# A graph network kernel on one core: 45 of the 99 groups of its dense stage moved beside two other stages

## The chip, the cores and the metric

The kernel runs on one core of a Trainium2 chip. The metric is the device time of one execution, in microseconds. The core has TensorE (PE, matmuls, and PEld, its weight loads), VectorE (DVE), ScalarE (ACT), GpSimd (POOL), SyncE (SP, which here only issues transfers) and 16 DMA engines. TensorE's clock has two levels, 1.2 and 2.4 GHz; the profile gives the granted clock as a share of the higher one.

## The reference

x holds 100,000 nodes of 64 features; 50,000 edges lead from src to dst, sorted by dst. Four layers follow one another, each of the form x = x + layer(relu(layernorm(x))):

- L0: attention with a weight matrix per node type and per edge type, softmax over the edges of a dst.
- L1: `relu(h_diff @ W_ffn.T + b_ffn)`, where h_diff sums differences of neighbours, gated by a cosine similarity, over edges.
- L2: `relu((h + agg) @ W0 + b0) @ W1 + b1` with a hidden width of 128.
- L3: attention over four heads, an output projection, `h @ Wf + bf`, and a layer norm with gamma and beta, added.

In each layer only nodes with an incoming edge receive a sum over edges; every other node gets what its own row gives. The kernel splits the work that way.

## The kernel before

The nodes, padded to 101,376, are 99 groups of 1024 rows; the padded edges are 99 groups of 512. Stages follow one another with a barrier between them: tables, dense, scores, softmax, attend, difference, propagate, mlp, heads. Each stage is a software pipeline written out per engine: in step n an engine works on group n for one operation and on group n - 1, n - 2 and so on for later ones (`st.back(lag)`). The order on each engine is the program's order; nothing reorders it. Buffers mostly come in threes (`U = 3`).

**dense** (L484) computes all layers for every node as if it had no edges, reads x and writes the normalized rows h2 and h3 (tables U2 and U3) and the output. Of a group, 128 partitions hold 8 rows of 64 each. The steps of group d: Pool adds the L1 bias row (x2, L517) and the L2 bias row (x2b, L520); VectorE sums and centers x2; ScalarE squares with an accumulator, row by row (L173), and takes the root; VectorE scales (h2, L193). TensorE turns h2 by four transposes (L655), ScalarE copies them to SBUF (L630), TensorE multiplies by w0, 64 rows of the array for each of two halves (the hidden layer, L673), ScalarE applies relu over both halves in one operation (L644), TensorE multiplies by w1 (m, L688). Two groups later: x3 = m + x2b (L582), normalized to h3, turned, copied (L633), multiplied by wf2 (h, L680, two column blocks per row); four groups later VectorE adds bias rows, normalizes and writes x4 (L565 to L613), with Pool's x3b (L530). Pool also scatters 396 index columns into the node table T0 there (L523), four per step.

**difference** (L1230), step n: Pool gathers four index columns of 128 rows (L1222). TensorE: p of group n - 2 (L1384), b of n - 2 (L1388, transposes), t of n (L1395, transposes of the gathered rows), c of n - 2 (L1401, eight passes of one column). VectorE: diff of n - 1 (L1298), lastv of n (L1304), the two scans (L1308, L1314), prod of n - 1 (L1318). ScalarE: relu of p, a square, a copy of b, a square, a copy of c. There are three PSUM banks for t.

**propagate** (L1409), step n: Pool gathers four columns (L1222), with a memset of a scratch tile between gathers (L1227). TensorE: t of n - 1 (L1528), f of n - 3 (L1533), x of n - 5 (L1538). VectorE: sum of n - 6, scan of n - 2 (L1473), centering, x2 of n - 4 (L1484), sum of squares, gating of n (L1491), reciprocal, scaling. ScalarE: square, root, relu of f, a store. There are three banks each for t and x.

TensorE, SP and Pool wait through a helper that is the same everywhere:

```python
def wait(eng, sem, value, passed=None):
...
    if isinstance(value, int) and value <= 0:
        return
    eng.wait_ge(sem, value)
```

## Time and profile before

| | us |
|---|---|
| median of 3 runs (6725.3 to 6734.1) | 6727.01 |
| the profiled execution | 6730.3 |
| its span, first to last instruction | 6728.5 |
| TensorE busy in the span | 5032.8 |
| VectorE busy | 4925.5 |
| Pool busy | 4927.1 |
| ScalarE busy | 2275.3 |

The profile is of one execution. A row of windows gives the stretch (us from the span's start), its length, the busy time of each engine with the number of instructions in parentheses, then the granted clock, the mean busy share of the DMA engines and GB/s. Where a row is of TensorE alone, only its busy time stands. A row of the timeline gives start, duration, engine, line, operation, tiles (out<-in), shapes, and in brackets the idle time before it with what ended it; for TensorE the shape 64*128 64x512 means 64 rows and 128 columns of the array and 512 moving columns. An fp32 matmul shows as two passes. A row of groups gives busy us, mean ns of one, and the idle time before. Starts that are closer than durations mean that operations overlap in their pipeline. No engine is busy over the whole span, so the table says little by itself; the stages have different limits.

### The profile page before, as it was taken

To read this page: it belongs to the slowest core of one execution; us is meant where nothing else is said; L and a number is where in the kernel's file an instruction comes from. 1 tells how busy PE (TensorE), PEld (TensorE's weight loads), DVE (VectorE), ACT (ScalarE), POOL (GpSimd) and SP (SyncE) were. 2 spreads that over 40 slices of the span, in tenths; PEclk is the share of its full clock that TensorE was granted. 3 is DMA by queue.
4 is the path that set the end of the run, shared out by engine and by line. 5 is a ranking of instruction groups with operands and counts; after the bars stand their busy time and mean duration, and the time that the engine had idled before them with its cause. 6 is when DMAs were issued, how large, how long until landed. Compare 5 with 4: busy or idle time off the path is not lost. (4 is left out here: it accounts for less than half of the span.)

```text
span 6728.5 us, 70067 instructions
## 1 busy us (share of the span) xinstructions
PE 5032.8 (75%) x17065; PEld 2608.6 (39%) x17065; DVE 4925.5 (73%) x7942; ACT 2275.3 (34%) x5856; POOL 4927.1 (73%) x5468
## 2 busy tenths in 40 slices
PE   0777777588888886888887888555578878788787
PEld 0455555344444442333334444122233334444443
DVE  4899999766676666999996666565567757666666
ACT  0555555322222222433332333121122223333333
POOL 1777777688888883666667887887677757777777
PEclk9877777799999997888885555555578867666666
DMA  9222222233333333555543333344455542222221
GB/s 350 88 95 95 95 95 95 78 75 78 74 79 74 78 75 81 142 145 143 145 130 83 83 82 77 93 109 102 100 136 144 146 119 62 65 65 65 62 61 42
DMA packets 788906, 673.39 MB, mean 100 GB/s; under 512 B 514176, under 2 KB 520906, under 8 KB 788376
## 3 DMA queue, kind: packets, MB, share of 16 engines
q1 hardware_dynamic: 486456, 459.62, 23.5%
q0 software_dynamic: 102464, 90.84, 8.5%
q10 hardware_dynamic: 199584, 118.45, 5.7%
q8 instruction: 145, 2.38, 0.1%
q14 instruction: 257, 2.11, 0.1%
HBM read 396.20 MB, written 276.35 MB: 100 GB/s over the span
## 5 line engine op out<-in xcount | busy, mean ns | idle before, releaser
L736 POOL DMA_INDIRECT sc_xg<-t,keep_gather x792 | 910.7, 1150 | 165.4 <-issue 146.4
L1222 POOL DMA_INDIRECT df_hs<-u,keep_idx x396 | 512.3, 1294 | 129.2 <-issue 108.3
L1222 POOL DMA_INDIRECT hd_gat<-u,keep_idx x396 | 478.5, 1208 | 161.6 <-issue 119.6
L1755 POOL DMA_INDIRECT out_x<-hd_x,keep_scat_out x396 | 458.1, 1157 | 151.4 <-issue 125.4
L1222 POOL DMA_INDIRECT ml_gat<-u,keep_idx x396 | 403.8, 1020 | 168.3 <-issue 70.0
L523 POOL DMA_INDIRECT t<-keep_ptr_pay,keep_scat_ptr x396 | 441.0, 1114 | 108.3 <-issue 106.1
L1222 POOL DMA_INDIRECT pr_gat<-sd,keep_idxsd x396 | 412.5, 1042 | 130.7 <-issue 69.4
L1198 PE MATMUL at_ps_m<-at_vx,keep_weights 128*64 128x512 f32 x792 | 447.3, 718 | 26.0 <-POOL at_vx L1095 26.0
L688 PE MATMUL den_ps_m<-keep_weights,den_hid 128*128 128x64 f32 x1584 | 243.8, 318 | 207.9 <-ACT den_hid L644 207.9
L876 PE MATMUL sc_ps_q<-sc_ht,keep_weights 128*128 128x512 f32 x396 | 272.7, 827 | 140.1 <-issue 84.9
L882 PE MATMUL sc_ps_r<-sc_qx,keep_weights 128*64 128x512 f32 x792 | 376.0, 619 | 1.0 <-DVE sc_prod L799 1.0
L1210 PE MATMUL at_ps_y<-keep_weights,at_agg 64*128 64x256 f32 x792 | 242.0, 456 | 170.8 <-DVE at_ysel L1122 170.6
L1095 POOL TENSOR_TENSOR at_vx<-at_eq,at_v 128x1024 f32<-128x1024 f32 x99 | 256.7, 2594 | 133.8 <-issue 81.2
L1895 PE MATMUL hd_ps_h<-keep_weights,hd_xb 128*128 128x128 f32 x792 | 249.3, 415 | 126.5 <-DVE hd_wn L1838 118.6
L150 DVE TENSOR_REDUCE sc_sc_n_sum<-sc_xg 128x8 f32<-128x512 f32 x99 | 67.9, 686 | 367.4 <-DMA sc_xg<-t,keep_gather 367.4
L154 DVE SCALAR_TENSOR_TENSOR den_den_n_cent<-den_den_n_sum,den_x 128x512 f32<-128x512 f32 x198 | 334.0, 1687 | 3.6
L655 PE MATMUL den_ps_t<-keep_consts,den_h 128*128 128x128 f32 x792 | 181.9, 380 | 197.0 <-DVE den_h L193 196.7
L688 PEld LDWEIGHTS den_ps_m<-keep_weights,den_hid 128*128 128x128 f32 x1584 | 228.3, 229 | 249.6 <-ACT den_hid L644 249.5
L1083 POOL TENSOR_TENSOR at_y<-at_ysel 128x512 f32<-128x512 f32 x99 | 137.3, 1387 | 245.4 <-DVE at_ysel L1122 245.4
L173 ACT ACTIVATE den_den_n_sq<-den_den_n_cent 128x64 f32<-128x64 f32 x792 | 190.6, 242 | 327.9 <-DVE den_den_n_cent L154 327.9
L1895 PEld LDWEIGHTS hd_ps_h<-keep_weights,hd_xb 128*128 128x128 f32 x792 | 196.7, 305 | 248.6 <-DVE hd_wn L1838 189.5
L833 ACT COPY sc_kv<-sc_ps_kv 128x512 f32<-128x512 f32 x99 | 58.1, 587 | 681.5 <-PE sc_ps_kv L888 672.9
(291 smaller groups left out, 13804.1 us busy)
## 6 DMA issues: line engine op xcount, KB each, us to landing
u<-den_h SPq DMA_DIRECT2D x198, 256.0 KB
t<-tab_row ACTq DMA_DIRECT2D x99, 272.0 KB, 11.3
tab_x<-in_x SPq DMA_DIRECT2D x99, 256.0 KB
den_x<-in_x SPq DMA_DIRECT2D x99, 256.0 KB
out_x<-den_x SPq DMA_DIRECT2D x99, 256.0 KB, 2.6
sc_et<-in_etype_row SPq DMA_DIRECT2D x99, 256.0 KB
at_v<-vt SPq DMA_DIRECT2D x198, 128.0 KB
at_et<-in_etype_row SPq DMA_DIRECT2D x99, 256.0 KB
```

Of the source, the lines that this page charges most:

```text
L154: v.scalar_tensor_tensor(out=self.cent[:, :, :], in0=self.over(self.sum), scalar=-1.0 / D, in1=x, op0=ALU.mult, op1=ALU.add).then_inc(self ...
L523: pool.indirect_dma_start(pairs, bass.IndirectOffsetOnAxis(ap=e.scat_ptr[:, c:c + 1], axis=0), e.ptr_pay[:, c, :], None, bounds_check=NP * ...
L688: m = pe.matmul(ps_m[:, j, :], hid[:, a, c * P:(c + 1) * P], e.W["w1"], start=(j == 0), stop=(j == RN - 1), skip_group_check=True)
L736: pool.indirect_dma_start(xg[i][:, u, :], None, e.T0, bass.IndirectOffsetOnAxis(ap=e.gather0[:, b.n, u:u + 1], axis=0), bounds_check=NP - ...
L876: m = pe.matmul(ps_q[:, :], e.W["q"][:, c * P:(c + 1) * P], ht[:, c, :], start=(c == 0), stop=(c == 1))
L882: m = pe.matmul(ps_r[:, :], e.W["att"][:, r * D:(r + 1) * D], qx[:, r, :], start=(r == 0), stop=(r == 3))
L1095: pool.tensor_tensor(vx[i][:, 2:4, :], eq[i][:, :, :], vin[i][:, :].unsqueeze(1).broadcast_to([P, 2, GE]), ALU.mult).then_inc(vx_high, 1)
L1198: m = pe.matmul(ps_m[d.s][:, :], e.W["msg"][:, r * D:(r + 1) * D], vx[d.s][:, r, :], start=(r == 0), stop=(r == 3))
L1210: m = pe.matmul(ps_y[:, u, :, :], agg[f.s][:, u * P:(u + 1) * P], e.W["a"][0:D, :].rearrange("p (t f) -> p t f", t=4), start=(u % 2 == 0), ...
L1222: pool.indirect_dma_start(gat[i][:, u, :], None, table, bass.IndirectOffsetOnAxis(ap=idx_all[:, c:c + 1], axis=0), bounds_check=rows - 1, ...
L1755: pool.indirect_dma_start(e.out, bass.IndirectOffsetOnAxis(ap=e.scat_out[:, c:c + 1], axis=0), x4[i][:, u, :], None, bounds_check=NP - 1, ...
L1895: pe.matmul(ps_h[i][:, u, :], xb[i][:, u * P:(u + 1) * P], e.W["wfx"], start=(u == 0), stop=False, skip_group_check=True)
```

## The change

Dense becomes a class whose work per group is cut into four parts per engine, with an own order of operations. It runs alone for 54 groups; 22 groups run beside difference and 23 beside propagate, one part per step of the host, at the end of each engine's step; what is left over runs after the host's last step. Pool has no arithmetic in dense: x2 and x2b go to VectorE; x3b and the bias of h's first block become matmuls with one row (`ones[0:1]` by `bias_h`) ahead of each half of h. VectorE sums the squares of x2; ScalarE squares in one wide operation and scales the rows of h2 and h3 by eight narrow operations each. The hidden layer has a bank per half. Beside a host (`tight`) both halves share one bank, as do the turns of h2 and h3. Difference and propagate keep one bank for t (and x) in place of three, so their waits go by the group before, not by the third before. In difference b, c and n share a bank. Pool's scatters spread over 54 steps, each let go by x2 of the step before; the memsets in propagate are gone.

```diff
+IN_DF = 22
+IN_PR = 23
...
+        dense(nc, e, NG - IN_DF - IN_PR)
...
+        difference(nc, e, NG - IN_DF - IN_PR, IN_DF)
+        propagate(nc, e, NG - IN_PR, IN_PR)
...
+                    link(v.tensor_copy(e.bias_h[0:1, :, half, :], bias[0:1, :].unsqueeze(1).broadcast_to([1, TU, D])))
...
+class Dense:
...
+    def __init__(self, s, e, first, count, tight=False):
...
+        self.ps_t2 = s.ps("dt2", [P, GE])
+        self.ps_t3 = self.ps_t2 if tight else s.ps("dt3", [P, GE])
+        self.ps_hid = [s.ps("dhid0", [P, GE])]
+        self.ps_hid.append(self.ps_hid[0] if tight else s.ps("dhid1", [P, GE]))
+        self.ps_m, self.ps_h = s.ps("dm", [P, RN, D]), s.ps("dh", [P, RN, 2, D])
...
+    def steps(self):
+        return self.count + 4
...
+    def vector(self, v, st, part):
+        e, d, f, g = self.e, st, st.back(2), st.back(4)
+        n2, n3, n4 = self.n2, self.n3, self.n4
+        if part == 0:
+            if self.on(f):
+                v.wait_ge(self.m_ready, f.n + 1)
+                v.wait_ge(self.x2b_done, f.n + 1)
+                wait(v, self.hx_done, f.n - (U - 1))
+                v.tensor_tensor(self.x3[f.s][:, :, :], self.ps_m[:, :, :], self.x2b[f.s][:, :, :], ALU.add).then_inc(self.x3_done, 1)
+            if self.on(g):
+                n4.sumsq(v, g)
+            if self.on(f):
+                v.wait_ge(self.x3_done, f.n + 1)
+                n3.total(v, self.x3[f.s][:, :, :]).then_inc(n3.chain, 1)
+            if self.on(d):
+                v.wait_ge(self.x_in[d.s], 16 * (d.k + 1))
+                v.tensor_tensor(self.x2[:, :, :], self.xin[d.s][:, :, :], self.rows(e.relu_b[:, :]), ALU.add).then_inc(self.x2_done, 1)
+        if part == 1:
+            if self.on(f):
+                v.wait_ge(n3.chain, 2 * f.n + 1)
+                wait(v, self.h3_done, f.n)
+                n3.shift(v, self.x3[f.s][:, :, :])
+            if self.on(g):
+                v.wait_ge(self.h_ready, g.n + 1)
+                wait(v, self.x4_done, g.n)
+                v.tensor_tensor(self.hx[:, :, :], self.ps_h[:, :, 1, :], self.x3[g.s][:, :, :], ALU.add).then_inc(self.hx_done, 1)
+                v.wait_ge(n4.rooted, g.n + 1)
+                v.reciprocal(n4.rstd[:, :], n4.std[:, :]).then_inc(n4.chain, 1)
+            if self.on(d):
+                v.wait_ge(self.x2_done, d.n + 1)
+                n2.total(v, self.x2[:, :, :]).then_inc(n2.chain, 1)
+            if self.on(g):
+                v.wait_ge(n4.chain, g.n + 1)
+                v.tensor_tensor(self.f1[:, :, :], self.ps_h[:, :, 0, :], n4.over(n4.rstd), ALU.mult).then_inc(self.f1_done, 1)
+        if part == 2:
+            if self.on(f):
+                n3.sumsq(v, f)
+            if self.on(d):
+                wait(v, self.x3_done, d.n - (U - 1))
+                v.tensor_tensor(self.x2b[d.s][:, :, :], self.x2[:, :, :], self.rows(e.W["b1_row"]), ALU.add).then_inc(self.x2b_done, 1)
+                v.wait_ge(n2.chain, 2 * d.n + 1)
+                wait(v, self.h2_done, d.n)
+                n2.shift(v, self.x2[:, :, :])
+            if self.on(f):
+                v.wait_ge(n3.rooted, f.n + 1)
+                v.reciprocal(n3.rstd[:, :], n3.std[:, :]).then_inc(n3.chain, 1)
+        if part == 3:
+            if self.on(g):
+                v.wait_ge(self.f1_done, g.n + 1)
+                v.tensor_tensor(self.f1[:, :, :], self.f1[:, :, :], self.rows(e.W["gamma"]), ALU.mult).then_inc(self.g1_done, 1)
+            if self.on(d):
+                n2.sumsq(v, d)
+            if self.on(g):
+                v.wait_ge(self.g1_done, g.n + 1)
+                v.wait_ge(self.hx_done, g.n + 1)
+                wait(v, self.x4_out[g.s], 16 * g.k)
+                v.tensor_tensor(self.x4[g.s][:, :, :], self.f1[:, :, :], self.hx[:, :, :], ALU.add).then_inc(self.x4_done, 1)
+            if self.on(d):
+                v.wait_ge(n2.rooted, d.n + 1)
+                v.reciprocal(n2.rstd[:, :], n2.std[:, :]).then_inc(n2.chain, 1)
+
+    def scalar(self, a, st, part):
+        e, d, f, g, d1, f1 = self.e, st, st.back(2), st.back(4), st.back(1), st.back(3)
+        eps = e.C["eps"]
+
+        def scale_rows(n, h, b, out, done):
+            a.wait_ge(n.chain, 2 * b.n + 2)
+            wait(a, out[b.s], 16 * b.k)
+            for j in range(RN):
+                m = a.activation(h[b.s][:, j, :], n.cent[:, j, :], ACT.Relu, scale=n.rstd[:, j:j + 1])
+            m.then_inc(done, 1)
+
+        if part == 0:
+            if self.on(g):
+                a.wait_ge(self.h_ready, g.n + 1)
+                wait(a, self.n4.summed, g.n)
+                a.activation(self.n4.sq[:, :, :], self.ps_h[:, :, 0, :], ACT.Square).then_inc(self.n4.squared, 1)
+                self.n4.root(a, g, eps)
+        if part == 1:
+            if self.on(f):
+                self.n3.square(a, f)
+            if self.on(d1):
+                a.wait_ge(self.t2, d1.n + 1)
+                a.copy(self.h2t[:, :], self.ps_t2[:, :]).then_inc(self.t2_kept, 1)
+            if self.on(f1):
+                a.wait_ge(self.t3, f1.n + 1)
+                a.copy(self.h3t[:, :], self.ps_t3[:, :]).then_inc(self.t3_kept, 1)
+        if part == 2:
+            if self.on(f):
+                self.n3.root(a, f, eps)
+            if self.on(d1):
+                for half in range(2):
+                    a.wait_ge(self.hid_ready, 2 * d1.n + half + 1)
+                    a.activation(self.hid[:, half, :], self.ps_hid[half][:, :], ACT.Relu, bias=e.W["b0"]).then_inc(self.hid_kept, 1)
+            if self.on(d):
+                self.n2.square(a, d)
+        if part == 3:
+            if self.on(f):
+                scale_rows(self.n3, self.h3, f, self.h3_out, self.h3_done)
+            if self.on(d):
+                self.n2.root(a, d, eps)
+                scale_rows(self.n2, self.h2, d, self.h2_out, self.h2_done)
+
+    def tensor(self, pe, st, part):
...
+        if part == 0:
+            if self.on(d):
+                wait(pe, self.h2_done, d.n + 1, passed)
+                wait(pe, self.t2_kept, d.n, passed)
+                if self.tight:
+                    wait(pe, self.t3_kept, f.n, passed)
+                turn(self.ps_t2, self.h2[d.s]).then_inc(self.t2, 1)
+        if part == 1:
+            if self.on(f):
+                wait(pe, self.h3_done, f.n + 1, passed)
+                wait(pe, self.t3_kept, f.n, passed)
+                if self.tight:
+                    wait(pe, self.t2_kept, min(d.n + 1, self.count), passed)
+                turn(self.ps_t3, self.h3[f.s]).then_inc(self.t3, 1)
+        if part == 2:
+            if self.on(d):
+                wait(pe, self.t2_kept, d.n + 1, passed)
+                for half in range(2):
+                    if self.tight:
+                        wait(pe, self.hid_kept, 2 * d.n + half, passed)
+                    else:
+                        wait(pe, self.hid_kept, 2 * (d.n - 1) + half + 1, passed)
+                    pe.matmul(self.ps_hid[half][:, :], e.W["w0"][64 * half:64 * half + 64, :],
+                              self.h2t[64 * half:64 * half + 64, :], start=True, stop=True).then_inc(self.hid_ready, 1)
+            if self.on(f):
+                wait(pe, self.t3_kept, f.n + 1, passed)
+                wait(pe, self.hx_done, f.n, passed)
+                wait(pe, self.f1_done, f.n, passed)
+                for bank in range(2):
+                    pe.matmul(self.ps_h[:, 4 * bank:4 * bank + 4, :, :], e.C["ones"][0:1, :], self.e.bias_h[0:1, :, :, :],
+                              start=True, stop=False, skip_group_check=True)
+                    for c in (2 * bank, 2 * bank + 1):
+                        m = pe.matmul(self.ps_h[:, 2 * c:2 * c + 2, :, :], self.h3t[:, c * P:(c + 1) * P],
+                                      e.W["wf2"], start=False, stop=(c % 2 == 1), skip_group_check=True)
+                m.then_inc(self.h_ready, 1)
+        if part == 3:
+            if self.on(d):
+                wait(pe, self.hid_kept, 2 * d.n + 2, passed)
+                wait(pe, self.x3_done, d.n, passed)
+                for j in range(RN):
+                    a, c = j % 2, j // 2
+                    m = pe.matmul(self.ps_m[:, j, :], self.hid[:, a, c * P:(c + 1) * P], e.W["w1"],
+                                  start=(j == 0), stop=(j == RN - 1), skip_group_check=True)
+                m.then_inc(self.m_ready, 1)
...
+class Hosted:
...
+    def beside(self, emit, n):
+        step, part = n // Dense.PARTS, n % Dense.PARTS
+        if step < self.den.steps():
+            emit(self.den.step(step), part)
+
+    def rest(self, emit, n):
+        for n in range(n, self.den.steps() * Dense.PARTS):
+            self.beside(emit, n)
+
+    def sync(self, sp, n):
+        if n % Dense.PARTS == 0 and n // Dense.PARTS < self.den.count + 6:
+            self.den.sync(sp, self.den.step(n // Dense.PARTS))
...
+def dense(nc, e, count):
...
+                for n in range(count):
+
+                    wait(pool, den.x2_done, n, e.pool_passed)
+                    for c in range(CH * n // count, CH * (n + 1) // count):
+                        pool.indirect_dma_start(pairs, bass.IndirectOffsetOnAxis(ap=e.scat_ptr[:, c:c + 1], axis=0),
+                                                e.ptr_pay[:, c, :], None, bounds_check=NP * TW // 2 - 1,
+                                                oob_is_err=False).then_inc(ptr_out, 16)
+                wait(pool, ptr_out, 16 * CH, e.pool_passed)
...
+def difference(nc, e, first, count):
...
-        ps_t = [s.ps(f"t{i}", [D, GE]) for i in range(U)]
...
+        ps_t, ps_p, ps_bcn = s.ps("t", [D, GE]), s.ps("p", [D, GE]), s.ps("bcn", [P, GE])
+        ps_b = ps_bcn[:, 0:TU * D].rearrange("p (u f) -> p u f", f=D)
+        ps_c, ps_n = ps_bcn[:, TU * D:TU * D + TU], ps_bcn[:, TU * D + TU:TU * D + TU + 2]
+        hosted = Hosted(Dense(s, e, first, count, tight=True))
...
+                    hosted.beside(lambda step, part: den.vector(v, step, part), st.n)
...
+                hosted.rest(lambda step, part: den.vector(v, step, part), NG + 1)
...
+                        wait(pe, c_kept, b.n, e.pe_passed)
...
-                        wait(pe, prod_done, st.n - (U - 1), e.pe_passed)
+                        wait(pe, prod_done, st.n, e.pe_passed)
...
-                        wait(pe, c_kept, b.n, e.pe_passed)
+                        wait(pe, b_kept, b.n + 1, e.pe_passed)
...
+                    hosted.beside(lambda step, part: den.tensor(pe, step, part), st.n)
...
+def propagate(nc, e, first, count):
...
-        ps_t, ps_x = [s.ps(f"t{i}", [D, GE]) for i in range(U)], [s.ps(f"x{i}", [P, TU, D]) for i in range(U)]
-        ps_f = s.ps("f", [D, GE])
+        ps_t, ps_f, ps_x = s.ps("t", [D, GE]), s.ps("f", [D, GE]), s.ps("x", [P, TU, D])
+        hosted = Hosted(Dense(s, e, first, count, tight=True))
...
-                    gather(pool, e.SD, e.idxsd, gat, gathered, st, st.n, EP, rest, rested)
+                    gather(pool, e.SD, e.idxsd, gat, gathered, st, st.n, EP)
...
-                        wait(pe, agg_done, d.n - (U - 1), e.pe_passed)
+                        wait(pe, agg_done, d.n, e.pe_passed)
...
-                        wait(pe, nrm.centered, x.n - (U - 1), e.pe_passed)
+                        wait(pe, nrm.centered, x.n, e.pe_passed)
```

SyncE runs `den.sync`, one load and three stores of a group, at the first part of each dense step; ScalarE's parts stand in the same places as TensorE's and VectorE's.

## Rows read from the trace of the kernel before

**Rows 1.** Windows: dense, difference, propagate; busy us of PE, PEld, DVE, ACT, POOL; PEclk, DMA

```profile
166.00:1301.00 1135.00, 832.06 (x3564) 572.02 (x3564) 1095.55 (x1683) 588.85 (x2377) 816.05 (x693) 0.78 0.28 93
...
3550.00:4201.00 651.00, 529.43 (x1784) 307.30 (x1784) 421.81 (x503) 209.15 (x696) 512.28 (x396) 0.50 0.32 81
4201.00:4841.00 640.00, 355.34 (x990) 130.80 (x990) 371.29 (x793) 133.44 (x298) 499.13 (x792) 0.50 0.43 102
```

**Rows 2.** Page: the granted TensorE clock in 40 slices of 168.2 us

```profile
PEclk9877777799999997888885555555578867666666
```

**Rows 3.** TensorE alone at 1.2 GHz: turn, hidden, h, m (dense), a 512-column pair (scores)

```profile
229.56:230.63 1.07, 1.07 (x6) 0.50 0.69 246
219.30:221.38 2.08, 2.08 (x6) 0.50 1.01 329
1289.98:1293.77 3.79, 3.78 (x8) 0.50 0.13 46
326.83:330.51 3.68, 3.68 (x17) 0.50 0.12 41
1367.74:1371.50 3.76, 3.76 (x5) 0.50 0.45 88
```

**Rows 4.** TensorE alone at 2.4 GHz: hidden, then h, in dense

```profile
442.87:444.01 1.14, 1.13 (x5) 1.00 0.67 241
444.17:446.14 1.97, 1.96 (x8) 1.00 0.73 239
```

**Rows 5.** One step of dense, TensorE alone: hidden, h, then m

```profile
1003.40:1005.41 2.01, 2.01 (x6) 0.50 0.97 309
1005.41:1008.73 3.32, 3.32 (x9) 0.58 0.04 14
1009.69:1011.69 2.00, 2.00 (x16) 0.98 0.01 0
```

**Rows 6.** Timeline of difference: start us, us, engine, line, operation; TensorE, VectorE, Pool

```profile
3701.83 1.97 PE L1384 MATMUL df_ps_p<-df_prod,keep_weights 64*64 64x512 f32 x2
3703.73 0.69 PE L1388 MATMUL df_ps_b<-keep_consts,df_sd 64*128 64x64 f32 x4
3704.35 1.06 PE L1395 MATMUL df_ps_t<-keep_consts,df_hs 128*64 128x128 f32 x4
3705.34 1.86 PE L1401 MATMUL df_ps_c<-keep_consts,df_act 64*128 64x1 f32 x8
...
3705.61 0.68 DVE L1298 TENSOR_TENSOR df_diff<-df_ps_t,df_hb 64x512 f32<-64x512 f32 x1 [1.07 <-issue]
...
3709.19 0.65 DVE L1318 TENSOR_TENSOR df_prod<-df_ps_t,df_hb 64x512 f32<-64x512 f32 x1
...
3702.77 2.00 POOL L1222 DMA_INDIRECT df_hs<-u,keep_idx  x1 [0.30 <-issue]
```

**Rows 7.** Timeline of dense: VectorE's wide operations, ScalarE's narrow ones

```profile
699.98 0.69 DVE L565 TENSOR_TENSOR den_den_n_cent<-den_ps_h,keep_bfo_cent 128x512 f32<-128x512 f32 x1
700.58 0.68 DVE L150 TENSOR_REDUCE den_den_n_sum<-den_x 128x8 f32<-128x512 f32 x1
...
704.28 0.24 ACT L173 ACTIVATE den_den_n_sq<-den_den_n_cent 128x64 f32<-128x64 f32 x1
704.42 0.19 ACT L173 ACTIVATION_READ_ACCUMULATOR den_den_n_sq<-den_den_n_cent 128x1 f32 x1
```

**Rows 8.** Groups of instructions in dense: busy us, mean ns, idle before

```profile
L523 POOL DMA_INDIRECT t<-keep_ptr_pay,keep_scat_ptr x396 | 441.0, 1114 | 108.3 <-issue 106.1
L154 DVE SCALAR_TENSOR_TENSOR den_den_n_cent<-den_den_n_sum,den_x 128x512 f32<-128x512 f32 x198 | 334.0, 1687 | 3.6
...
L166 ACT ACTIVATE den_den_n_sq<-den_den_n_cent 128x512 f32<-128x512 f32 x198 | 123.8, 625 | 8.4 <-DVE den_den_n_cent L154 5.4 <-DVE den_den_n_cent L565 3.0
```

**Rows 9.** Timeline of propagate, TensorE: first and last piece of a step

```profile
4503.57 1.06 PE L1528 MATMUL pr_ps_t<-keep_consts,pr_gm 128*64 128x128 f32 x4 [0.18 <-issue]
...
4506.45 0.69 PE L1538 MATMUL pr_ps_x<-keep_consts,pr_x 64*128 64x64 f32 x4
```

More of the change, by code:

```diff
@@ L501, in dense @@
[L501 to L503 removed]
+        den = Dense(s, e, 0, count)
+        ptr_out = s.sem("ptr_out")
         with nc.Block() as block:
@@ L649, in _ @@
-                run_groups(a, body, U, 4)
+                for n in range(den.steps()):
+                    for part in range(den.PARTS):
+                        den.scalar(a, den.step(n), part)
             @block.tensor
             def _(pe):
-                def turn(ps, rows):
-                    for c in range(4):
-                        m = pe.transpose(ps[:, c * P:(c + 1) * P], rows[:, 2 * c:2 * c + 2, :].rearrange("p a f -> p (a f)"),
-                                         e.C["ident"])
-                    return m
@@ L691, in _ @@
-                run_groups(pe, body, U, 4)
+                for n in range(den.steps()):
+                    for part in range(den.PARTS):
+                        den.tensor(pe, den.step(n), part)
 def scores(nc, e):
@@ L1369, in body @@
                         a.copy(e.gate[:, bass.ds(pos(b) * TU, TU)], ps_c[:, :]).then_inc(c_kept, 1)
+                    hosted.beside(lambda step, part: den.scalar(a, step, part), st.n)
                 a.wait_ge(cleared, 1)
                 run_groups(a, body)
+                hosted.rest(lambda step, part: den.scalar(a, step, part), NG + LAST)
                 a.wait_ge(n_ready, 1)
@@ L1498, in body @@
                         c.end()
+                    hosted.beside(lambda step, part: den.vector(v, step, part), st.n)
                 run_groups(v, body, U, 6)
+                hosted.rest(lambda step, part: den.vector(v, step, part), NG + 6)
             @block.scalar
@@ L1514, in body @@
                         a.dma_start(edge_rows(e.U2, g.n * GE), h2[g.s][:, :, :]).then_inc(h2_out[g.s], 16)
+                    hosted.beside(lambda step, part: den.scalar(a, step, part), st.n)
                 run_groups(a, body, U, 6)
+                hosted.rest(lambda step, part: den.scalar(a, step, part), NG + 6)
                 for i in range(U):
```

274 lines of the change are left out of this document (80 added, 194 removed).

## The prediction

> **What bounds the kernel now.** I read the stretches by stage first, then the granted clock in the page's slices, then the timelines. Dense takes 1135.0 us with VectorE busy for 1095.55 of them: VectorE bounds it [rows 1]. Difference (651.0 us) and propagate (640.0 us) are paced by Pool, which is busy 512.28 and 499.13 us with only its issue gaps between gathers, while TensorE is busy 529.43 and 355.34 us, VectorE 421.81 and 371.29 us [rows 1]. That idle time is what the hosted groups are to fill. The column to see is PEclk: 0.78 in dense, but 0.50, that is 1.2 of 2.4 GHz, over the whole of difference and of propagate [rows 1, 2]. So TensorE's 529.43 us in difference are 81% of the stage at the low level, and it has only 121.6 us to spare; in propagate 284.7 us.
>
> **TensorE's price per dense group.** At 1.2 GHz: four transposes 1.07 us, both halves of the hidden layer 2.08, the eight passes of h 3.79, the sixteen of m 3.68 [rows 3]. At 2.4 GHz hidden and h take 1.14 and 1.97 [rows 4], m 2.00 [rows 5]. New are two bias matmuls per group (K = 1, 512 columns each). The trace has none with one row; two 128-row matmuls of 512 columns took 3.76 us at the low level [rows 3], and I take that, since the moving columns are the same. The other end is 0.69 us, what four 64-column passes take (L1388 [rows 6]), should one row stream far faster; that end would take 54 x 3.07 = 166 us off dense and 45 x 3.07 = 138 off the other two. Beside another stage (tight) the two halves of hidden share a bank: each goes alone, as L1384 does in 1.97 us [rows 6], with ScalarE's copy of some 0.75 us between (0.62, as for the same width in rows 8, and two handovers). A group at the low level so costs 1.07 + 1.07 + 2.08 + 3.76 + 3.79 + 3.68 = 15.4 us in dense's own stage and 1.07 + 1.07 + 1.97 + 0.75 + 1.97 + 3.76 + 3.79 + 3.68 = 18.1 us beside.
>
> **Which level the clock will have.** In the stretch before a rise, TensorE streams hidden (both halves) and then h without a gap, 128 rows of the array in use; the rise comes within h, and m then runs at 0.98 [rows 5]. In difference TensorE also works without a gap through p, b, t and c from 3701.83 us on, but with 64-row operands and one-column matmuls, and the whole stage stays at 0.50 [rows 1, 6]. The Trainium skill (TensorE: Matmul & The Clock Gate, Part 1) says that the default is throttled and sustained activity releases it; this trace agrees in dense but not for those 64-row stretches. By that rule alone the fuller TensorE would run difference and propagate at 2.4 GHz, which is a rival below. The change makes the stretch that raised the clock worse: a one-row bias matmul stands ahead of each half of h, and, as the walk below shows, a gap opens ahead of hidden. I take 0.50 in dense, difference and propagate.
>
> **Dense alone, 54 groups.** VectorE's 14 wide operations start 0.60 us apart [rows 7], 8.4 us and three reciprocals: it no longer bounds. L154, 1687 ns on the mean with Pool's adds beside it [rows 8], should come down to the 0.68 of its neighbours [rows 7]. Pool keeps 396 scatters of 1114 ns and 0.27 us of issue, 549 us, 10.2 us a step [rows 8], covered. TensorE's path sets the step. When m ends, VectorE does x3, sumsq4, total3, x2, shift3 (5 x 0.60 + 0.1), ScalarE square3 (0.62 [rows 8]) and the copy of t2 (0.6), so hidden starts about 4.5 us after m's end; the two turns (2.1 us) lie under that, with a gap of over 2 us before hidden. Then 2.08 + 3.76 + 3.79 + 3.68: a step of 17.8 us. 52 full steps are 926 us, the incomplete ones and the ends some 65: 991, against 1135.0. **-144 us.** Bounds: TensorE without a gap, 54 x 15.4 = 832 (-303); no gain (0).
>
> **Difference, 22 groups.** Own work of a step on TensorE: p 1.90, b 0.62, t 1.0, c 1.8, start to start [rows 6]; VectorE from diff's start to prod's end 4.2 us [rows 6]. ps_t is now one bank, so t(n+1) waits for prod(n), and VectorE's part of step n lies ahead of that on its engine. ScalarE reaches its part only after copying c's result. Part by part, from c's end to the next c's end: part 0: square4 and its wait 0.9, sumsq4, total3, x2 1.8, own 4.2, t and c 2.8, so 9.8 us (TensorE's own chain would be 6.4). Part 1: TensorE 1.4 waiting for t2_kept, turn 1.07, own 5.3: 7.8. Part 2: hidden 4.7, bias and h 7.5, own 5.3: 17.5. Part 3: scale_rows 1.6 (eight of 0.24 at most, 0.15 apart at least [rows 7]), root and reciprocal 0.5, own 4.2, t and c 2.8: 9.2 (TensorE: m 3.68 + 5.3 = 9.0). Together 44.3 us for four steps. Of 26 dense steps 20 are full, 886 us; the six incomplete ones 177, start and end 15: 1078 us. **+427 us.** Lower bound, TensorE never waiting: 529.43 + 22 x 17.3 (the copy's 0.75 filled) = 910 (+259).
>
> **Propagate, 23 groups.** TensorE's own step is 3.57 us from t's start to x's end [rows 9], VectorE's 371.29 / 99 = 3.75 us [rows 1]. Part 0, from the start of VectorE's step: its scan done at 1.7, then t and f 2.9 of the 3.57, ScalarE's relu of f 0.7, square4 0.65, and sumsq4, total3, x2 1.85: 7.8. Part 1: VectorE's own 4.1 with its waits and 2.5 of dense: 6.6. Part 2: TensorE 3.6 + 12.2 = 15.8. Part 3: 3.6 + 3.7, of which 7.2 are left. Together 37.4 us for four steps. 21 full ones 785 us, the rest 155 and 10: 950 us. **+310 us.** Lower bound 355.34 + 23 x 17.3 = 753 (+113).
>
> **At nothing or nearly.** The memsets gone from propagate free Pool, but Pool no longer paces. Its gathers may get slower beside a fuller VectorE: one beside VectorE's scans took 2.00 us, with an issue gap of 0.30 [rows 6]. Were every gather 2.30 us, a step would be 9.2 us and the stage 911 us, under my 1078 and 950: it decides nothing at the low clock. The SP queue gets dense's four transfers (one load, three stores) at every fourth step, behind waits on results one or more dense steps old, and the hosting stages' own loads run one to two steps ahead: free while that lead lasts. The two copies into bias_h: +1 us.
>
> **Sum.** 6728.5 - 144 + 427 + 310 + 1 = 7322.5 span; the profiled execution took 6730.3, 1.8 more than its span and 3.3 over the median of 6727.01. So 7324 for it and 7321 for the median; I say **7320**. All lower bounds together: 6727 - 303 + 259 + 113 = 6796: at 0.50 in all three stages no overlap, however good, makes it faster.
>
> **Rivals.** *Bias counts, B:* the one-row matmuls keep the clock as 128-row ones would. Then the rise comes some 5 us after hidden's start, as in rows 5, and dense's step is 4.5 + 4.9 + 4.3 = 13.7 us: 772 us, 219 less; beside the others some 1.5 us per group, 68 less: 7035. For it: the same columns move. Against: the 64-row stretches of rows 6. *Good overlap, O:* the waits I walked are hidden by the two or three buffers of each stage, or the bias passes are short; half way from 7324 to the bound is 7060. *Full clock, F, faster:* TensorE's added work lifts difference and propagate to 2.4 GHz. Dense's step is 4.5 + 1.14 + 1.96 + 1.97 + 2.00 = 11.5 us (-475), difference, by the same walk with TensorE's pieces halved, 7.8 us a step (826, +175), propagate 6.4 from VectorE's 3.9 + 2.5 (690, +50): 6480. It decides only where the clock rises in all three; with dense alone raised, 7324 - 331 = 6993, still slower. The Trainium skill's rule above would give F. Against: not one of propagate's or difference's slices shows over 5 tenths [rows 2]. *Worse, W:* more waits than walked, over 7500.
>
> **How the numbers follow.** My case (7150 to 7500) 0.60, B and O together 0.22, W 0.06, F or dense raised with near perfect overlap 0.10, near zero 0.02. From no change, about 0.2% can be told. Range 6990 to 7500: it takes in my case, B and O, and leaves F and W out. Faster 0.10, same 0.02, slower 0.88.
>
> **What would show it.** Right: PEclk 0.5 over all of dense, difference and propagate; dense 54 groups at 17 to 18 us; TensorE over 85% busy in difference; the long steps in every fourth (part 2, near 17 us). Wrong: a clock over 0.6 in dense (B), bias passes shorter than 0.9 us, Pool's gathers back to back in difference.

## The result, and the profile after

The changed kernel took 7288.51 us (median of 4 runs, 7283.56 to 7303.9) against 6726.16 for the kernel before on the same chip (6722.63 to 6734.1): a ratio of 1.084, 95% interval [1.082, 1.086]. 562 us slower, and 31 us under the 7320 of the prediction.

The windows of the three stages in the changed kernel answer to [rows 1] (busy us of PE, PEld, DVE, ACT, POOL, then PEclk, DMA share, GB/s):

```profile
core 0: us, PE busy (x) PEld busy (x) DVE busy (x) ACT busy (x) POOL busy (x), PEclk, DMA share, GB/s
166.00:1149.00 983.00, 804.71 (x2160) 478.24 (x2160) 482.63 (x918) 469.88 (x1405) 399.92 (x396) 0.58 0.18 59
3391.00:4467.00 1076.00, 917.12 (x2664) 509.08 (x2664) 611.94 (x876) 395.22 (x1268) 487.45 (x396) 0.50 0.26 70
4467.00:5406.00 939.00, 745.70 (x1910) 341.95 (x1910) 576.09 (x1184) 330.34 (x896) 429.57 (x396) 0.51 0.37 95
```

Dense lost 152 us (983 for 1135), difference gained 425 (1076 for 651), propagate 299 (939 for 640). VectorE, which bounded dense, is busy 482.63 of 983 us; TensorE took its place with 804.71, and is at 85% in difference and 79% in propagate. The clock column: dense fell from 0.78 to 0.58, the other two stay at 0.50 and 0.51. The page's slices show the same, to be read against [rows 2]; the 9 and 8 at the left edge precede the first record of the clock and stand for nothing (hidden takes 2.08 us there too), and they lift the 0.58. In the middle of dense, 400 to 800 us, the clock is 0.52, against 0.77 for the same stretch before:

```profile
PEclk9855557999999788886555555555558777767766
```

A step of dense, TensorE's rows (start us, us, engine, line, operation, idle before and its releaser), with [rows 5] as its counterpart:

```profile
703.83 2.08 PE L677 MATMUL den_ps_dhid<-den_dh2t,keep_weights 64*128 64x512 f32 x4 [2.60 <-ACT den_dh2t L625]
705.84 2.07 PE L684 MATMUL den_ps_dh<-keep_bias_h,keep_consts 1*128 1x512 f32 x2
707.83 2.07 PE L687 MATMUL den_ps_dh<-keep_weights,den_dh3t 128*128 128x256 f32 x4
709.84 2.07 PE L684 MATMUL den_ps_dh<-keep_bias_h,keep_consts 1*128 1x512 f32 x2
711.84 2.08 PE L687 MATMUL den_ps_dh<-keep_weights,den_dh3t 128*128 128x256 f32 x4
713.71 3.51 PE L696 MATMUL den_ps_dm<-keep_weights,den_dhid 128*128 128x64 f32 x16
717.01 1.92 PE L651 MATMUL den_ps_dt<-keep_consts,den_dh 128*128 128x128 f32 x8
721.53 1.22 PE L677 MATMUL den_ps_dhid<-den_dh2t,keep_weights 64*128 64x512 f32 x2 [2.60 <-ACT den_dh2t L625]
```

Hidden to hidden is 17.70 us. Each bias matmul with one row (2.07 us) takes as long as its half of h with 128. Before the change m ran behind a rise of the clock, in 2.00 us at 0.98 [rows 5]; in this step nothing rises, and m takes 3.51. The 0.52 is not quite 0.50 because 9 of the 54 steps do have a short rise somewhere (m then takes 2.71 at the least).

From four steps of difference, the long one without its b and t:

```profile
3811.98 1.04 PE L1486 MATMUL df_ps_t<-keep_consts,df_hs 128*64 128x128 f32 x4 [3.34 <-DVE df_prod L1404]
...
3820.68 1.86 PE L1492 MATMUL df_ps_bcn<-keep_consts,df_act 64*128 64x1 f32 x8
3822.40 2.05 PE L677 MATMUL df_ps_dhid<-df_dh2t,keep_weights 64*128 64x512 f32 x2
3825.23 2.07 PE L677 MATMUL df_ps_dhid<-df_dh2t,keep_weights 64*128 64x512 f32 x2 [0.78 <-ACT df_dhid L635]
3827.23 2.07 PE L684 MATMUL df_ps_dh<-keep_bias_h,keep_consts 1*128 1x512 f32 x2
3829.23 2.07 PE L687 MATMUL df_ps_dh<-keep_weights,df_dh3t 128*128 128x256 f32 x4
3831.23 2.07 PE L684 MATMUL df_ps_dh<-keep_bias_h,keep_consts 1*128 1x512 f32 x2
3833.23 2.08 PE L687 MATMUL df_ps_dh<-keep_weights,df_dh3t 128*128 128x256 f32 x4
3835.24 1.97 PE L1474 MATMUL df_ps_p<-df_prod,keep_weights 64*64 64x512 f32 x2
...
3838.74 1.86 PE L1492 MATMUL df_ps_bcn<-keep_consts,df_act 64*128 64x1 f32 x8
```

From c to c this long step is 18.06 us, of which TensorE idles 0.78. In another of the four it waits 3.34 us for prod. Pool, which paced the stage before, now waits for TensorE (columns: busy us and mean ns, then idle before and what ended it):

```profile
L1304 POOL DMA_INDIRECT df_hs<-u,keep_idx x396 | 487.4, 1231 | 555.2 <-PE df_ps_t L1486 431.4 <-issue 111.6 <-POOLq L210 8.7
```

### The profile page after: what moved, and what is told of

It reads as the page before. It is cut to its first block and busy times, and to the rows that moved or that the text cites. A ratio compares the mean times of both kernels' runs of the same rounds, so it can differ in the third digit from the quotient of the medians.

```text
span 7281.8 us, 70259 instructions
## 1 busy us (share of the span) xinstructions
PE 5771.2 (79%) x17461; PEld 2926.2 (40%) x17461; DVE 4714.1 (65%) x7944; ACT 2539.1 (35%) x6054; POOL 4415.2 (61%) x4775
## 5 line engine op out<-in xcount | busy, mean ns | idle before, releaser
L1304 POOL DMA_INDIRECT df_hs<-u,keep_idx x396 | 487.4, 1231 | 555.2 <-PE df_ps_t L1486 431.4
L746 POOL DMA_INDIRECT t<-keep_ptr_pay,keep_scat_ptr x396 | 399.9, 1010 | 636.8 <-DVE den_dx L558 399.5
L1304 POOL DMA_INDIRECT pr_gat<-sd,keep_idxsd x396 | 429.6, 1085 | 485.0 <-DVE pr_gm L1585 329.6
L550 DVE TENSOR_TENSOR den_dx<-den_ps_dm,den_dx2b 128x512 f32<-128x512 f32 x54 | 37.4, 692 | 383.1 <-PE den_ps_dm L696 373.2
L1233 DVE TENSOR_TENSOR_SCAN at_agg<-at_same,at_agg,at_am 64x512 f32<-64x512 f32 x98 | 282.2, 2880 | 0.0
L859 DVE SCALAR_TENSOR_TENSOR sc_qx<-sc_et,keep_consts,sc_ps_q 128x512 f32<-128x512 int32 x396 | 276.8, 741 | 7.3 <-PE sc_ps_r L964 7.3
L1292 PEld LDWEIGHTS at_ps_y<-keep_weights,at_agg 64*128 64x128 f32 x792 | 165.5, 219 | 218.8 <-issue 192.0
L1955 ACT COPY hd_ht<-hd_ps_t 64x512 f32<-64x512 f32 x99 | 57.2, 578 | 549.8 <-PE hd_ps_t L2005 277.1
```

What stands on the lines that cost most here:

```text
L746: pool.indirect_dma_start(pairs, bass.IndirectOffsetOnAxis(ap=e.scat_ptr[:, c:c + 1], axis=0), e.ptr_pay[:, c, :], None, bounds_check=NP * ...
L859: return v.scalar_tensor_tensor(out=qx[:, r, :], in0=et[b.s][:, :], scalar=e.C["rels"][:, r:r + 1], in1=ps_q[:, :], op0=ALU.is_equal, op1= ...
L1233: v.tensor_tensor_scan(agg[i][:, :], same[i][:, :], am[:, :], 0.0 if b.first() else agg[(i - 1) % U][:, GE - 1:GE], ALU.mult, ALU.add).the ...
L1292: m = pe.matmul(ps_y[:, u, :, :], agg[f.s][:, u * P:(u + 1) * P], e.W["a"][0:D, :].rearrange("p (t f) -> p t f", t=4), start=(u % 2 == 0), ...
L1304: pool.indirect_dma_start(gat[i][:, u, :], None, table, bass.IndirectOffsetOnAxis(ap=idx_all[:, c:c + 1], axis=0), bounds_check=rows - 1, ...
```

## Experiments

They ran on other chips of the same kind, where the kernel before takes 6615 to 6623 us instead of 6726; a total is therefore read as its ratio to the kernel before on its own chip, and a stage against the first run below. The border of difference and propagate is put at VectorE's first instruction of propagate, 7 us later than above.

**The two kernels again.** No edit.

> The changed kernel itself, on the chip of the other runs, where the kernel before took 6620.8 instead of 6726.2. If the chips differ only in what paces difference, propagate and mlp before (Pool's gathers; mlp took 595 instead of 663 in four runs), the changed kernel, paced by TensorE in the two hosting stages, gains only mlp's 68 less 26 in scores: about 7230 to 7250, and difference and propagate stay at 1076 and 939 within 15. If every stage is faster there: about 7175 (the ratio 1.0838 kept).

> The kernel before with a profile on the same chip: 6621. Dense 1135 as before and mlp 595; then the 64 us that are left of the difference between the chips, 106 - 68 + 26, lie in difference and propagate: 1291 - 64 = 1227 for both, against 590 + 558 = 1148 for both with nothing hosted beside them and without Pool's memsets.

Measured: 7205.28 us for the changed kernel, ratio 1.088 [1.086, 1.089]; 6621.28 for the kernel before. Windows of the changed one, then difference and propagate of the one before:

```profile
166.00:1136.00 970.00, 804.44 (x2160) 478.01 (x2160) 482.29 (x918) 470.01 (x1405) 399.87 (x396) 0.57 0.19 59
3396.00:4479.00 1083.00, 917.43 (x2664) 509.73 (x2664) 612.29 (x878) 395.45 (x1268) 493.15 (x402) 0.50 0.27 71
4479.00:5395.00 916.00, 751.76 (x1910) 345.98 (x1910) 575.64 (x1183) 330.34 (x896) 424.16 (x391) 0.50 0.38 97
```

```profile
3566.00:4223.00 657.00, 528.81 (x1784) 306.74 (x1784) 421.65 (x502) 209.52 (x696) 517.38 (x405) 0.50 0.33 81
4223.00:4814.00 591.00, 353.66 (x990) 130.61 (x990) 367.93 (x793) 129.23 (x298) 493.55 (x784) 0.50 0.48 109
```

Dense before is again 1135. The chips differ in mlp (593 here, 670 there), propagate (591, 632) and, the other way, scores (1294, 1274). Difference of the changed kernel is the same on both (1083 on this cut). My 7230 to 7250 was too high, since its dense and propagate came out some 15 us shorter each. Why chips differ was not tried.

**All 99 groups alone.** IN_DF and IN_PR set to 0, so the stages keep their single banks and host nothing. Hosted work also kept the norm's matmul of difference away from the last copy of c, so a wait says it here:

```diff
-IN_DF = 22
-IN_PR = 23
+IN_DF = 0
+IN_PR = 0
...
                 wait(pe, tot_done, 1, e.pe_passed)
+                wait(pe, c_kept, NG, e.pe_passed)
```

> All 99 groups alone in dense by the new code, none beside difference and propagate, which keep their single PSUM banks (and one wait for the last copy of c ahead of the norm's matmul). Theory 1 (the hosted work itself lengthens the two stages, the single banks do not): difference and propagate come back to 651 and 640 within 15 us, dense takes 983 + 45 x 17.7 = 1780; in all about 7290 - 425 - 299 + 797 = 7363. Theory 2 (the single banks lengthen them): difference or propagate stays 50 us or more above 651 or 640, in all over 7400.

Measured 7143.66, ratio 1.079 [1.077, 1.081]. Dense, difference, propagate:

```profile
166.00:1928.00 1762.00, 1475.51 (x3960) 876.82 (x3960) 882.13 (x1683) 860.30 (x2575) 407.44 (x396) 0.53 0.18 60
4192.00:4782.00 590.00, 529.60 (x1784) 307.52 (x1784) 425.84 (x503) 203.77 (x696) 446.35 (x401) 0.50 0.36 90
4782.00:5340.00 558.00, 351.28 (x990) 130.94 (x990) 375.42 (x792) 139.38 (x298) 409.38 (x391) 0.50 0.51 116
```

A group alone costs 1762 / 99 = 17.8 us. Hosted it costs (1083 - 590) / 22 = 22.4 us in difference and (916 - 558) / 23 = 15.6 in propagate. So the three stages take 2969 us hosting and 2910 not: beside propagate a group is 2.2 us cheaper than alone, beside difference 4.6 dearer, and the overlap as a whole is worth less than nothing. And both host stages are *shorter* than before the change when nothing is hosted, which neither theory had; the next two runs take that up.

**The stage edits alone.** The kernel before, with its own dense, and of the change only the single banks and the missing memsets (with the same wait for c_kept as above):

> The kernel before with nothing of the change but the single PSUM banks of difference and propagate and Pool's memsets gone from propagate; dense is that of before, nothing is hosted. Theory 1 (in the run with all groups alone, difference took 590 against 657 and propagate 558 against 591 because of these two edits): the same here, 67 + 33 = 100 us less: 6520, ratio 0.985, dense 1135. Rival (the shorter stages there came from what ran ahead, not from the edits): 6620, difference 657.

Measured 6510.18 (5 runs), ratio 0.985 [0.983, 0.986]: faster than both kernels. Then one edit per stage:

```diff
 difference:
-        ps_t = [s.ps(f"t{i}", [D, GE]) for i in range(U)]
+        ps_t = s.ps("t", [D, GE])
...
-                        wait(pe, prod_done, st.n - (U - 1), e.pe_passed)
+                        wait(pe, prod_done, st.n, e.pe_passed)
 propagate:
-                    gather(pool, e.SD, e.idxsd, gat, gathered, st, st.n, EP, rest, rested)
+                    gather(pool, e.SD, e.idxsd, gat, gathered, st, st.n, EP)
```

> The kernel before with one edit per stage: in difference ps_t alone becomes one bank (b, c and the norm keep their own), in propagate Pool's memsets alone go (two banks of t and x stay). Theory 1 (the one bank of ps_t, by making the transposes wait for prod, moves Pool's gathers against VectorE's scans, so that fewer of them take 2 us; in propagate the memsets are the cost): difference 586 to 590 instead of 657, propagate 554 to 558 instead of 591: in all 6510 to 6525. Rivals: the shared bank of b, c and n did it, difference 657; the single banks did it in propagate, 591 there.

Measured 6513.35, ratio 0.985 [0.983, 0.987]. (Propagate keeps three banks each of t and x here, not the two of the expectation.) Difference and propagate of this run:

```profile
3565.00:4150.00 585.00, 529.12 (x1784) 307.07 (x1784) 422.50 (x503) 203.62 (x696) 443.06 (x401) 0.50 0.37 91
4150.00:4708.00 558.00, 353.67 (x990) 130.59 (x990) 367.52 (x793) 129.22 (x298) 411.33 (x392) 0.50 0.50 116
```

The single bank of ps_t takes 72 us off difference by itself, and the memsets are worth 33 us of propagate: with one between them, two gathers lie 0.38 us apart, without it 0.30, and 396 times 0.08 is 32. How the single bank helps, the gathers of difference tell: before, then with it (the page, busy us and mean ns).

```profile
L1222 POOL DMA_INDIRECT df_hs<-u,keep_idx x396 | 511.6, 1292 | 129.1 <-issue 96.0
```

```profile
L1222 POOL DMA_INDIRECT df_hs<-u,keep_idx x396 | 438.3, 1107 | 129.0 <-issue 119.7
```

Pool's queue is full in both; the gathers themselves got shorter, by 73.3 us in all, which is the stage's gain. Counted in the timelines, 95 of the 396 gathers of the kernel before take 1.8 us or more and 55 take 1.25 to 1.8; with the single bank 92 take 1.4 to 1.5, 6 more, and the other 298 near 1.00. Every gather over 1.1 us overlaps VectorE's scans for 0.9 us or more, in both. What differs is where they start: before, mostly right behind the start of the second scan; with the single bank, in the middle of the first. Before, then with the single bank:

```profile
3799.82 1.25 DVE L1314 TENSOR_TENSOR_SCAN df_hb<-df_same,df_hb,df_lastv 64x512 f32<-64x512 f32 x1
3799.88 2.00 POOL L1222 DMA_INDIRECT df_hs<-u,keep_idx  x1 [0.30 <-issue]
```

```profile
3803.08 1.27 DVE L1308 TENSOR_TENSOR_SCAN df_sd<-df_same,df_sd,df_diff 64x512 f32<-64x512 f32 x1
3803.74 1.42 POOL L1222 DMA_INDIRECT df_hs<-u,keep_idx  x1 [0.30 <-issue]
```

The timelines say more than this. A gather over 1.1 us that starts while a scan runs ends 0.80 to 0.82 us after the end of that scan, in all 98 such cases before and all 97 with the single bank: it lasts as long as the rest of the scan and 0.8 us, so 2.00 with 1.2 us of scan left and 1.42 with 0.6 left. (Twelve gathers before and one after start within 0.07 us of a scan's start and take only 1.00.) So a wait that fixes where the transposes, and with them the scans, fall moves the gathers out of the worst place. That the place does it is read from the timelines; it was not moved by itself.

**Bias with 128 rows.** The same two matmuls and columns, the other 127 rows zero:

```diff
-        e.bias_h = keep.sb("bias_h", [1, TU, 2, D])
+        e.bias_h = keep.sb("bias_h", [P, TU, 2, D])
...
+                link(v.memset(e.bias_h[:, :, :, :], 0.0))
...
-    pe.matmul(..., e.C["ones"][0:1, :], self.e.bias_h[0:1, :, :, :],
+    pe.matmul(..., e.C["ones"], self.e.bias_h[:, :, :, :],
```

> Theory 1 (the clock stays at 1.2 GHz in dense because the one-row bias matmuls break the stretch of 128-row work): with the same passes on 128 rows the clock rises in each step during h as it did before the change; dense's step goes from 17.7 to about 13.7 us, its stage from 983 to about 770, clock over 0.7; some 1.5 us less per hosted group, difference 1076 to about 1045, propagate 939 to about 905; in all about 7290 - 280 = 7010. Theory 2 (the gap of 2.6 us ahead of hidden keeps the clock down, the rows do not matter): dense at 0.58 and 983 as before, in all 7290 +-15. Theory 3 (one-row matmuls are cheaper than 128-row ones, so the edit costs): over 7300.

Measured 6826.76, ratio 1.031 [1.030, 1.033]. The three stages:

```profile
166.00:931.00 765.00, 558.77 (x2160) 355.23 (x2160) 482.34 (x918) 464.65 (x1405) 400.48 (x396) 0.76 0.23 75
3197.00:4185.00 988.00, 779.40 (x2664) 446.97 (x2664) 612.15 (x877) 395.07 (x1268) 497.28 (x401) 0.58 0.29 78
4185.00:5020.00 835.00, 629.70 (x1910) 298.51 (x1910) 575.88 (x1184) 330.37 (x896) 425.21 (x391) 0.59 0.42 106
```

and a step of its dense:

```profile
499.26 2.08 PE L678 MATMUL den_ps_dhid<-den_dh2t,keep_weights 64*128 64x512 f32 x4 [3.42 <-ACT den_dh2t L626]
501.26 2.07 PE L685 MATMUL den_ps_dh<-keep_bias_h,keep_consts 128*128 128x512 f32 x2
503.13 1.91 PE L688 MATMUL den_ps_dh<-keep_weights,den_dh3t 128*128 128x256 f32 x4
504.84 1.17 PE L685 MATMUL den_ps_dh<-keep_bias_h,keep_consts 128*128 128x512 f32 x2
505.85 1.03 PE L688 MATMUL den_ps_dh<-keep_weights,den_dh3t 128*128 128x256 f32 x4
506.71 1.89 PE L697 MATMUL den_ps_dm<-keep_weights,den_dhid 128*128 128x64 f32 x16
508.44 1.04 PE L652 MATMUL den_ps_dt<-keep_consts,den_dh 128*128 128x128 f32 x8
```

Passes, columns and order are those of the changed kernel; only the rows are filled, and the clock rises in the first half of h. It does so in nearly every step: m takes less than 2.3 us in 52 of the 54, in the changed kernel in none. The step is 13.65 us, dense 970 to 765 as expected. This settles theory 1: it is the rows, the gap ahead of hidden is even longer here (3.42 us). Beside the other stages the edit is worth 95 and 81 us, where I had written 31 and 34: TensorE gets 138 us of difference back, 6.3 per group, as m, which follows one host step later, also runs at 2.4 GHz (2.05 us for 3.68), and so do the second half of h and the host's own step behind it. The total of 7010 was missed by 183 us: 111 are those two stages, most of the rest is that 7010 was counted from 7290, where these chips give 7205.

**No bias at all.** The two matmuls removed, h's first matmul opening each bank.

> Leaves out the bias matmuls (the output part h lacks its bias). Theory 1 (one-row matmuls neither count for the clock nor come free, but TensorE's path sets the step): 4.1 us of 1.2 GHz time go from each dense step, and with h straight behind hidden the clock rises as before the change: 54 x (17.7 - 10.5 to 13) , dense 983 to 600 or 720, below the 765 of the 128-row bias; beside, 45 x 4.1 = 185 us less and some rises in the fourth step: difference 1076 to 960, propagate 939 to 820. In all 6750 to 6850. Theory 3 (their own time is the whole harm, the clock stays down): dense 983 - 221 = 762 at a clock of 0.55 to 0.6, in all about 6870.

Measured 6678.75, ratio 1.008 [1.006, 1.010], below the 6750 to 6850 expected. Dense 693 us at 0.77, difference 963 at 0.54, propagate 786 at 0.58. From the 970 of this chip dense lost 277 us; the passes' own time is 221 of them (54 x 4.1), so their time is the larger part of the harm and the clock the other 56. Even so the kernel is no faster than the one before.

**ScalarE's copies first.**

```diff
         if part == 1:
-            if self.on(f):
-                self.n3.square(a, f)
             if self.on(d1):
                 a.wait_ge(self.t2, d1.n + 1)
                 ...
+            if self.on(f):
+                self.n3.square(a, f)
```

> ScalarE's copies of t2 and t3 go ahead of its square of x3. Theory 1 (TensorE's chain sets dense's step, with the wait ahead of hidden, 2.6 us, in it): the wait goes, step 17.7 to about 15.1 at 1.2 GHz, 54 x 2.6 = 140 us off dense (983 to 843); beside difference and propagate 1 to 2 us off each fourth step, 45 x 1 = 45 and more: in all about 7105. If closing the gap also lets the clock rise for the stretch turn, turn, hidden: step 12 to 14, dense 650 to 760. Theory 2 (VectorE's and ScalarE's chain from m's end over square3 to scale_rows sets the step): the copies only put square3 off, dense 983 or more, in all 7290 or more.

Measured 7102.57, ratio 1.073 [1.071, 1.075]. The expected total was counted from 7290, not from this chip's 7205, so its hit is chance: dense fell 90 us (970 to 880), not 140, difference 11, propagate 0. The 2.60 us ahead of hidden shrank to 0.47, but 0.86 us of waiting for f1 (VectorE) came up ahead of the bias: a step without a rise went from 17.7 to 16.5 us, some 67 us in all. The other 23 or so are short rises: 19 of the 54 steps have one, for 8 in the changed kernel's run above, and the clock from 400 to 800 us is 0.54 for 0.51. So closing the gap raised the clock a little, and nowhere near what filled rows do.

**Both edits**, the filled rows and the copies first, their diffs as above.

> Both edits: the bias matmuls on 128 rows, the copies first. Theory 1 (rows and gap each matter): TensorE streams 128-row work without a break, so the clock is at 2.4 GHz in most of dense: step 8.4 to 11 us (VectorE's 14 wide operations and three reciprocals, or TensorE's 0.66 + 0.66 + 1.14 + 2 + 2 + 2 = 8.5), dense 480 to 620 instead of 983. Beside difference and propagate the clock rises in the long fourth step: 3 to 5 us less per group, 130 to 220 us. In all 6700 to 6900. Theory 2 (only one of the two matters): the same as the better of the other two edits, 7010 to 7105.

Measured 6737.68, ratio 1.018 [1.016, 1.019]; dense 673 at 0.86, not the 480 to 620 expected. With the clock up another loop sets the step, 11.9 us on the mean: x3, six operations of VectorE up to f1, bias and h on the banks that f1 frees, m, x3. In difference and propagate it gives nothing over the filled rows (987 and 835). Hosting does not pay here either: against the 590 and 558 of the run with nothing hosted a group costs 18.0 and 12.0 us beside the two stages, 12.5 (673 / 54) alone. That is an estimate, as both edits with all groups alone and the old order were not run.

**Alone, VectorE's order changed**, with both edits: x3 and what follows from it behind f1.

```diff
         if part == 0:
-            if self.on(f):
-                ... x3 = ps_m + x2b, total3
...
         if part == 1:
-            if self.on(f):
-                ... shift3
...
                 ... f1 = ps_h * rstd4
+            if self.on(f):
+                ... x3 = ps_m + x2b, total3, shift3
```

> All 99 groups alone, bias on 128 rows, copies of t2 and t3 first, and VectorE's work put so that f1, which frees the banks of h, comes ahead of x3. Theory 1: with the rows and the gap mended the clock is at 2.4 GHz, and the loop f1 - bias - h - m - x3 (12 us in the run with the first two edits) is cut: step 9.2 (VectorE) to 10.5 us, dense 950 to 1070 for 99 groups, with difference and propagate at 590 and 558: in all 6330 to 6450, faster than the kernel before (6621). Rival: another wait takes its place (scale_rows to the turns), step 11.5 to 12: dense 1180, in all 6560, about the same as before.

Measured 6735.25, ratio 1.017 [1.015, 1.018], dense 1354, outside both expectations and worse per group (13.7) than both edits with the old order. By the timeline it now hung on ScalarE's queue, where the square of h stood behind the scaling of h2: VectorE waits 2.6 us a step for that square, TensorE's turns 2.9 for the scaling. **Then ScalarE's order too**: relu of hidden ahead of the square of x3, the square of h ahead of the scaling of h2. VectorE's order changed with it: the sum of that square goes to the end of the step before, x2 and the centering of x2 come earlier. So the run does not part the two engines.

```diff
         if part == 0:
-            ... square4, root4 (g)
         if part == 1:
-            self.n3.square(a, f)
             ... copy t2, copy t3
         if part == 2:
-            self.n3.root(a, f, eps)
             ... relu of hidden
+            self.n3.square(a, f)
             self.n2.square(a, d)
+            self.n3.root(a, f, eps)
         if part == 3:
             scale_rows(self.n3, ...)
             self.n2.root(a, d, eps)
+            ... square4 (f1)
             scale_rows(self.n2, ...)
+            self.n4.root(a, f1, eps)
```

> All 99 groups alone, bias on 128 rows; ScalarE does hidden's relu ahead of the square of x3 and the square of h behind scale_rows of h3; VectorE does f1 ahead of x3 and the sum of squares of h at the end of the step. Theory 1 (ScalarE's in-order queue, 9.2 us of work with waits in it, was what held the step at 13.4 us in the run before): step 10.0 to 10.6 us, dense 1040 to 1100, in all 6420 to 6480, below the kernel before. Rival (some 12 us loop is left, or the clock falls back to 1.2 GHz since the busy share sinks): dense over 1200, in all over 6580.

Measured 6547.06, ratio 0.990 [0.988, 0.991], dense 1164 at 0.83. Neither 1040 to 1100 nor over 1200: the new dense comes within 29 us of the old one's 1135, and no further. The gain over the kernel before is that of the stage edits.

**ScalarE's hosted part ahead of c** in parts 0 and 3 of difference.

```diff
+                    ahead = st.n % Dense.PARTS in (0, 3)
+                    if ahead:
+                        hosted.beside(lambda step, part: den.scalar(a, step, part), st.n)
                     if b.on():
                         a.wait_ge(c_ready, b.n + 1)
                         ...
-                    hosted.beside(lambda step, part: den.scalar(a, step, part), st.n)
+                    if not ahead:
+                        hosted.beside(lambda step, part: den.scalar(a, step, part), st.n)
```

> In difference ScalarE does its hosted part ahead of the copy of c in every fourth step's parts 0 and 3. Theory 1 (in part 0 VectorE's hosted work, and so prod and the next t, waits for ScalarE's square of h, which stands behind c on ScalarE): the wait of 3.3 us ahead of t in part 0 goes, 22 x 3 = 65 to 75 us off difference (1083 to about 1010), nothing elsewhere: about 7205 - 70 = 7135. Rival (another wait ends last in these steps): within 15 us of 7205.

Measured 7147.28, ratio 1.081 [1.079, 1.082]; difference 1028 for 1083. The wait for prod on TensorE (total us, times, longest), in the changed kernel and in this one:

```profile
PE df_ps_t L1486 <- DVE df_prod L1404: 92.6, 44, 4.4
```

```profile
PE df_ps_t L1490 <- DVE df_prod L1404: 40.8, 24, 4.4
```

Over half of it goes, 52 of the 55 us that the stage gains: the wait was where the walk had put it, worth 2.5 us a group instead of 3.3.

## Why the prediction was right

**The account.** On these chips the 584 us between the two kernels divide into: stage edits -100 (590 and 558 from 657 and 591), dense's new code +627 (1762 from 1135, all alone), hosting 45 of the groups +59 (2969 from 2910). The sum is 586. Against the forecast, on its own chip: -152, +425 and +299 for -144, +427 and +310, 21 us less in all, and the stages that the change leaves alone, put at nothing, came out 19 us shorter (scores and mlp 7 each, heads 5); the cause is open. The errors are small because the walks were right step by step, and in one place by luck, as told under difference.

**Bound and clock.** The premise held: at 0.50 to 0.52 in all three stages TensorE has no room for 45 groups. The reason given for it, that 128-row work raises the clock and one-row or 64-row work doesn't, is now shown for the one-row matmuls: filling the rows alone brought dense's clock to 0.76 and its time to 765 us, against the 772 that rival B would have given, had they counted. The second reason, the gap ahead of hidden, was not needed: with filled rows the clock rose in spite of it, and closing it alone took the clock from 0.51 to 0.54. B's price beside the other stages, 68 us, was too low; it measured 176.

**TensorE's price.** The 3.76 us for the bias pair measured 4.1, the far end of 0.69 is ruled out. 15.4 us a group alone: 804.71 / 54 = 14.9. 18.1 beside: (917.4 - 529.6) / 22 = 17.6 in difference, (751.8 - 351.3) / 23 = 17.4 in propagate.

**Dense.** Step 17.8, measured 17.70; stage 991, measured 983; "over 2 us" ahead of hidden is 2.60. VectorE's centering, with Pool's adds gone from beside it, fell from 1687 to 686 ns on the mean, as forecast.

**Difference.** 44.3 us for four steps against 45.2 (t at 3802.25 to t at 3847.41); 1078 against 1076. The four parts, put at 9.8, 7.8, 17.5 and 9.2, are 9.7, 7.7, 18.1 and 9.6; part 0's wait for prod was there, and scale_rows takes 2.02 us instead of 1.6. That the stage is hit within 2 us is luck: 20 full steps are 17 us over the walk, the incomplete ones and the ends 19 under their round figures.

**Propagate.** 37.4 for four steps, 37.5 measured; 950 against 939.

**At nothing.** "Pool no longer paces" held for the changed kernel, where Pool idles 431.4 us for t. But I costed the memsets and the single bank only as part of it and did not ask what they do with Pool still in the lead. That is the step that failed: I counted the single bank of t as a wait added and nothing else, where by itself it takes 72 us off a stage that Pool bounds. It cost the forecast nothing, as hosting buried it, but with the memsets it was the one useful part of the change.

**Rivals.** F fell: TensorE is busy 85% of difference and the clock stays at 0.50. The rule of the Trainium skill behind F (TensorE: Matmul & The Clock Gate, Part 1), that activity as such releases the throttle, does not hold for this stage. O and W did not come about.

## What to carry to other kernels

Idle time of an engine is room for other work only at the clock that the stage has: difference, 81% busy at 1.2 GHz, had a full engine, and moved work brought its full price and waits on top (22.4 us a group, 17.6 of them TensorE's work); propagate, 60% busy, hid little of it (15.6 for 17.4). A one-row matmul that adds a bias costs as much time as a 128-row one and can also hold the clock down for what follows; fill the rows with zeros, or add the bias elsewhere. When a change has several parts, time the ones that were only meant to make room: here they alone gave 1.5%, and the rest made 10% of loss on top (a ratio of 1.088 against 0.985).

## What was not expected of the hardware

- Only the number of rows in use changed between two kernels with the same matmuls, and the granted clock of dense went from 0.52 to 0.75 (both from 400 to 800 us), that of difference and propagate from 0.50 to 0.58 and 0.59.
- One PSUM bank for t instead of three made a stage 72 us faster, by way of gathers that fell from 1292 to 1107 ns on the mean.
- A gather on Pool takes 1.00 us by itself; if it starts while VectorE runs a scan, it nearly always ends 0.8 us after that scan: 1.42 us with 0.6 of the scan left, 2.00 with 1.2 left.
- The same program differs by 1.6% between chips (6726 and 6621 us), in other stages up as well as down, while ratios keep to half a per cent (1.084 and 1.088).
